# Expert tiles of a two-layer graph and mixture-of-experts kernel, as two halves of 128 rows with an expert each

## What is computed

```python
x = x + L0_gnn(layernorm(x), adj, ...)      # spectral graph block, with the eigenvectors of a 64x64 matrix
x = x + L0_ffn(layernorm(x), ...)           # 8 experts, the best two for each token
x = x + L1_gnn(layernorm(x), adj, ...)      # graph block with two batch norms
x = x + L1_ffn(layernorm(x), ...)           # a shared expert, and 8 experts, the best two for each token
# L0_ffn, for an expert e with 341 hidden units, silu and a gate product:
#   y = (silu(t @ w1[e].T) * (t @ w3[e].T)) @ w2[e].T
# L1_ffn, for an expert e with 512 hidden units, gelu and biases:
#   y = gelu(t @ W1p[e] + b1p[e]) @ W2p[e] + b2p[e]
# out[token] = gate1 * y[expert1] + gate2 * y[expert2]
```

## Time and profile before

| | |
|---|---|
| median of 3 runs | 1552.71 us (1551.8 to 1555.42) |
| the profiled execution's own time | 1541.83 us |
| its span on the core | 1540.1 us, mean granted TensorE clock 0.888 |
| PE busy | 1131.8 us (73%), weight loads 943.4 us |
| DVE busy | 917.6 us (60%) |
| ACT busy | 599.5 us (39%) |
| POOL busy | 629.1 us (41%) |
| expert part of layer 0 | 448 to 835 us |
| expert part of layer 1 | 1162 to 1506 us |

### The profile page before, as it was taken

How to read it: one execution, slowest core, us unless ns; L and a number is a source line. 1 busy time by engine, 2 the same in 40 slices (tenths; PEclk the granted TensorE clock), 3 DMA queues, 4 the chain that set the end, 5 groups by cost and what they waited for, 6 DMA issues and landing times.

```text
span 1540.1 us, 23912 instructions
## 1 busy us (share of the span) xinstructions
PE 1131.8 (73%) x6500; PEld 943.4 (61%) x6500; DVE 917.6 (60%) x3700; ACT 599.5 (39%) x1665; POOL 629.1 (41%) x611
## 2 busy tenths in 40 slices
PE   4555774688635449999996777887886339999991
PEld 3555663466524338888886434665655229999990
DVE  5776888678852126666675868756532115555673
ACT  3556554144400002222222784655432004444440
POOL 2000000334566655555544400223455665666664
PEclk9999999988756669999998898988898569999996
DMA  9991000001121112222343400000011112222446
GB/s 235 428 429 81 1 1 1 1 10 36 40 62 53 53 47 64 64 63 61 92 120 92 186 1 14 15 18 25 30 52 45 48 56 70 73 73 69 122 114 218
DMA packets 59268, 125.57 MB, mean 82 GB/s; under 512 B 13132, under 2 KB 39637, under 8 KB 57600
## 3 DMA queue, kind: packets, MB, share of 16 engines
q0 software_dynamic: 20000, 73.21, 12.7%
q1 hardware_dynamic: 39136, 50.84, 12.0%
HBM read 50.83 MB, written 74.99 MB: 82 GB/s over the span
## 4 chain that ended last, share of the span: by engine, by line
PE 58%; DVE 16%; another core or an unknown queue 9%; issue 7%; ACT 6%; DMA 2%; SPq 0%; POOL 0%; DVEq 0%; ACTq 0%; POOLq 0%
PE bank L1473 14%; PE bank L1464 8%; PE bank L1462 6%; PE bank L1461 6%; PE bank L1679 4%; PE bank L1687 4%; PE bank L195 3%; PE bank L389 3%; PE bank L1449 2%; PE bank L1634 2%; ACT work L1568 2%; DMA u<-planes 1%; PE bank L859 1%; DVE u L180 1%
## 5 line engine op out<-in xcount | busy, mean ns | idle before, releaser
L1326 POOL DMA_INDIRECT planes<-work,goal x284 | 309.4, 1089 | 279.1 <-DVE work L1385 221.8
L1473 PE MATMUL bank<-pay 128*128 128x128 f32 (+1 forms) x1988 | 289.1, 286 | 93.7 <-issue 48.5
L973 POOL DMA_INDIRECT rows<-pay,slot x256 | 253.2, 989 | 240.1 <-issue 174.5
L1473 PEld LDWEIGHTS bank<-pay 128*128 128x128 f32 (+1 forms) x1988 | 269.3, 197 | 114.2 <-issue 53.4
L1433 ACT ACTIVATE pay<-bank,pay 128x256 f32<-128x256 f32 x284 | 125.2, 475 | 219.5 <-PE bank L1464 109.9
L1429 ACT ACTIVATE pay<-bank 128x256 f32<-128x256 f32 (+1 forms) x213 | 81.6, 383 | 322.1 <-PE bank L1462 191.8
L1406 DVE TENSOR_TENSOR pay<-pay,bank 128x256 f32<-128x256 f32 (+1 forms) x213 | 89.0, 418 | 111.2 <-issue 62.2
L1464 PE MATMUL bank<-pay 128*128 128x256 f32 x568 | 140.3, 392 | 17.5 <-issue 16.2
L1461 PE MATMUL bank<-pay 128*128 128x256 f32 (+1 forms) x426 | 134.4, 398 | 12.1 <-issue 12.1
L1462 PE MATMUL bank<-pay 128*128 128x256 f32 (+1 forms) x426 | 132.9, 395 | 0.0
L1464 PEld LDWEIGHTS bank<-pay 128*128 128x128 f32 x568 | 105.9, 197 | 31.2 <-issue 17.5
(11 more groups left out here) (406 smaller groups left out, 1978.7 us busy)
## 6 DMA issues: line engine op xcount, KB each, us to landing
rows<-pay POOLq DMA_DIRECT2D x10, 3432.0 KB, 56.0
pay<-rows SPq DMA_DIRECT2D x142, 130.0 KB
u<-planes SPq DMA_DIRECT2D x64, 256.0 KB, 4.9
planes<-work,goal POOLq DMA_INDIRECT x284
wreg<-in_w SPq DMA_DIRECT2D x1, 4264.0 KB, 24.6
wreg<-in_w SPq DMA_DIRECT2D x1, 4112.0 KB, 13.4
X<-in_x SPq DMA_DIRECT2D x2, 2048.0 KB, 20.3
rows<-pay,slot POOLq DMA_INDIRECT x256
```

Source lines behind the costliest of these rows:

```text
L973: return self.nc.gpsimd.indirect_dma_start(out=xs, out_offset=bass.IndirectOffsetOnAxis(ap=self.t["slot"][:, k, q:q + 1], axis=0), in_=sel ...
L1326: nc.gpsimd.indirect_dma_start(out=planes, out_offset=bass.IndirectOffsetOnAxis(ap=t["goal"][:, j * 2 + h:j * 2 + h + 1], axis=0), in_=t[" ...
L1473: ins = T.matmul(ps[4 + j % 2][:, h * P:(h + 1) * P], t["hh"][c][0:n, h * P:(h + 1) * P], t["wst"][j % 2][0:n, at + c * P:at + (c + 1) * P ...
```

## The change

A tile keeps its 256 rows, but they are now two halves of 128 rows, each with its own expert, first row and number of real rows. A break of an expert's rows then costs part of 128 rows rather than part of 256. The worst case is 135 halves, so NT is 68 in place of 71, in both layers. PURE becomes 28 (25 before), FIRSTS 36 (39), EARLY 51 (54), which is NT - 17 as before.

- SP loads a tile by two DMAs of 128 rows, one row to a partition, with two register loads.
- The weight buffers `wst` hold two experts. In layer 0 DVE copies the first half's weights and ACT the second half's; in layer 1 DVE makes both copies, and both copies of the second bias. The second of the two buffers lies in the region `u1`, where the fetched planes now have 8 places in place of 16.
- The first products have 128 columns in place of 256, and twice as many of them. The second products, which were 128 wide already, keep their number.
- In layer 1 a Gelu covers 128 columns, and there are two for each chunk, since their bias columns differ. The Silus of layer 0 stay at 256.
- `table` counts in halves. Its comparison of 24 x 32 elements and the reduction of it are replaced by three operations on 24 elements that round up; other operations go over 2 x 24 elements.

```diff
-TS = 256
+TS = 2 * P
-NT = (2 * TOKENS + E8 * (TS - 1)) // TS
+HALVES = (2 * TOKENS + E8 * (P - 1)) // P
+NT = -(-HALVES // 2)
...
-PURE = -(-(TOKENS - E8 * (TS - 1)) // TS)
-FIRSTS = (TOKENS + E8 * (TS - 1)) // TS
-EARLY = 54
+PURE = -(-(TOKENS - E8 * (P - 1)) // P) // 2
+FIRSTS = -(-((TOKENS + E8 * (P - 1)) // P) // 2)
+EARLY = NT - 17
+YB = 8
...
-        cmp = tb["cmp"][:, 0:n * 32].rearrange("p (e i) -> p e i", i=32)
-        own.chain(V.tensor_tensor(cmp, count.unsqueeze(2).to_broadcast([P, n, 32]),
-                                  iota.unsqueeze(1).to_broadcast([P, n, 32]), ALU.is_gt))
-        own.chain(V.tensor_reduce(k, cmp, AX.X, ALU.add))
...
+        own.chain(V.tensor_scalar(k, count, 1.0 / P, (P - 1.0) / (2 * P), ALU.mult, ALU.add))
+        own.chain(V.tensor_scalar(k, k, WHOLE, None, ALU.add))
+        own.chain(V.tensor_scalar(k, k, WHOLE, None, ALU.subtract))
...
 def experts_sp(nc, sp, S, t, route, xs, planes):
...
-        at = sp.value_load(t["first"][j:j + 1, 0:1], min_val=0, max_val=E8 * CAP - TS)
+        ats = [sp.value_load(t["first"][j:j + 1, h:h + 1], min_val=0, max_val=E8 * CAP - P) for h in range(2)]
...
-        sp.dma_start(t["xin"][j % 4], xs[bass.ds(at, TS), :].rearrange("(p h) c -> p (h c)", h=2)
-                     ).then_inc(s(f"xin{j % 4}"), 16)
+        for h in range(2):
+            sp.dma_start(t["xin"][j % 4][:, h * ROW:(h + 1) * ROW], xs[bass.ds(ats[h], P), :]
+                         ).then_inc(s(f"xin{j % 4}"), 16)
...
 def experts_dve(nc, dve, own, S, t, ps, route):
     def weights(j):
...
+        if layer == 0:
+            expert = dve.value_load(t["expert"][j:j + 1, 0:1], min_val=0, max_val=E8 - 1)
+            V.tensor_copy(t["wst"][j % 2][:, 0, 0:WB[0]], W[:, bass.ds(expert * WB[0], WB[0])]).then_inc(s("w"), 1)
+            return
+        if j >= 2:
+            dve.wait_ge(s("biased"), j - 1)
+        for h in range(2):
+            expert = dve.value_load(t["expert"][j:j + 1, h:h + 1], min_val=0, max_val=E8 - 1)
+            V.tensor_copy(t["wst"][j % 2][:, h, WB[1]:WST[1]], t["b2p"][:, bass.ds(expert * P, P)]).then_inc(s("b2"), 1)
+            V.tensor_copy(t["wst"][j % 2][:, h, 0:WB[1]], W[:, bass.ds(expert * WB[1], WB[1])]).then_inc(s("w"), 1)
...
-def experts_act(nc, act, S, t, ps, layer):
+def experts_act(nc, act, S, t, ps, route):
+    def weights(j):
+        expert = act.value_load(t["expert"][j:j + 1, 1:2], min_val=0, max_val=E8 - 1)
+        if j >= 2:
+            act.wait_ge(s("down"), past("down", j - 1))
+        A.copy(t["wst"][j % 2][:, 1, 0:WB[0]], t["W"][:, bass.ds(expert * WB[0], WB[0])]).then_inc(s("second_w"), 1)
...
     for j in range(NT):
+        if layer == 0 and j + 1 < NT:
+            weights(j + 1)
...
-                A.activation(t["hh"][c], ps[c][:, 0:TS], ACT.Gelu,
-                             bias=t["wst"][j % 2][:, 2 * CH1 * P + c:2 * CH1 * P + c + 1]).then_inc(s("hh"), 1)
+                for h in range(2):
+                    ins = A.activation(t["hh"][c][:, h * P:(h + 1) * P], ps[c][:, h * P:(h + 1) * P], ACT.Gelu,
+                                       bias=t["wst"][j % 2][:, h, 2 * CH1 * P + c:2 * CH1 * P + c + 1])
+                ins.then_inc(s("hh"), 1)
...
     def up(j, c):
...
+            if layer == 0:
+                pe.wait_ge(s("second_w"), j + 1)
...
-            T.matmul(ps[c][0:n, 0:TS], w[:, a:a + n], x, start=True, stop=True)
-            T.matmul(ps[c][0:n, TS:2 * TS], w[:, HID0 + a:HID0 + a + n], x, start=True, stop=True).then_inc(s("up"), 1)
-        else:
-            T.matmul(ps[c][:, 0:TS], w[:, c * P:(c + 1) * P], x, start=True, stop=True).then_inc(s("up"), 1)
+        a, n = CH0[c] if layer == 0 else (c * P, P)
+        for h in range(2):
+            ins = T.matmul(ps[c][0:n, h * P:(h + 1) * P], w[:, h, a:a + n], x[:, h * P:(h + 1) * P], start=True, stop=True)
+            if layer == 0:
+                ins = T.matmul(ps[c][0:n, TS + h * P:TS + (h + 1) * P], w[:, h, HID0 + a:HID0 + a + n],
+                               x[:, h * P:(h + 1) * P], start=True, stop=True)
+        ins.then_inc(s("up"), 1)
```

More of the change, by code:

```diff
@@ L1015, in table @@
+        own.chain(V.tensor_copy(f[:, E8:n], k[:, 0:2 * E8]))
+        own.chain(V.tensor_tensor(k, k, f, ALU.subtract))
         own.chain(V.tensor_tensor_scan(end, self.t["ones"][:, 0:n], k, 0.0, ALU.mult, ALU.add))
+        own.inc(V.tensor_tensor(left, both(end), half, ALU.is_gt))
         own.chain(V.tensor_tensor(start, end, k, ALU.subtract))
-        own.inc(V.tensor_scalar(m, start, j, None, ALU.is_le))
-        if self.split:
-            own.chain(V.tensor_tensor(start, start, f, ALU.subtract))
@@ L1020, in table @@
-        own.chain(V.tensor_scalar(u, start, -float(TS), j256, ALU.mult, ALU.add))
-        own.chain(V.scalar_tensor_tensor(out=m, in0=end, scalar=j, in1=m, op0=ALU.is_gt, op1=ALU.mult))
-        whole = each_part(count[:, n - E8:n])
-        own.inc(V.tensor_tensor(by_part(k), whole, by_part(u), ALU.subtract))
-        own.chain(V.tensor_tensor(by_part(u), by_part(u), base, ALU.add))
-        own.inc(V.tensor_tensor(k, k, m, ALU.mult))
-        own.inc(V.tensor_tensor(u, u, m, ALU.mult))
-        own.chain(V.tensor_tensor(by_part(e), number, by_part(m), ALU.mult))
@@ L1028, in table @@
-        own.chain(V.tensor_reduce(tb["v"], k, AX.X, ALU.add))
-        V.tensor_scalar(tb["diag"], self.t["ident"], tb["v"], None, ALU.mult).then_inc(s("limits"), 1)
+        own.inc(V.tensor_tensor(m, both(start), half, ALU.is_le))
+        own.chain(V.tensor_tensor(k, start, f, ALU.subtract))
+        own.inc(V.tensor_tensor(m, m, left, ALU.mult))
+        own.chain(V.tensor_tensor(u, half, both(k), ALU.subtract))
+        own.inc(V.scalar_tensor_tensor(out=by_part(left), in0=by_part(u), scalar=-float(P), in1=each_part(count[:, 2 * E8:n]),
+                                       op0=ALU.mult, op1=ALU.add))
@@ L1887, in build @@
         t["OUT1"] = U1[:, :]
-        t["yb"] = [pairs(U1[:, T * TOK:(T + 1) * TOK]) for T in range(TILES)]
+        t["yb"] = [pairs(U1[:, T * TOK:(T + 1) * TOK]) for T in range(YB)]
         t["WS"] = W[:, E8 * WB[1]:E8 * WB[1] + WSH]
@@ L1960, in layer_view @@
             v["slot"] = slot[:, layer, :, :]
[L1961 removed]
+            v["first"], v["expert"] = ints[:, layer, 0:2], ints[:, layer, 2:4]
             v["goal"] = goal[:, layer, :]
```

135 lines of the change are left out of this document (66 added, 69 removed).

## The result

The changed kernel takes 1582.32 us, median of 4 runs (1577.0 to 1584.32), against 1554.07 us before, median of 4 (1551.8 to 1555.82): ratio 1.0177, 95% interval 1.0146 to 1.0209. It is 28 us slower where 10.6 us less were forecast, and lies outside the range.

What follows compares the result with a forecast made beforehand. PE was taken to bound the tiles outside the sends' stretch. Layer 0's -7.9, layer 1's -5.0, starts' +0.9 and +0.4 and the sends' +1.0 make -10.6 us: 1552.7 to 1542.1 us, range 1534 to 1560.

Steps and rivals of the forecast that it cites:

- Part 1: Both layers: three tiles fewer make 63 steps 60, saving 12.7 and 11.2 us, 23.9 us in all.
- Part 2: First products of 128 columns on PE: +0.08 us a tile in layer 0 (4.305), +0.055 in layer 1 (3.785).
- rival C: PE's first products: the added weight loads cost time; 0.25 of the surcharge makes 1549 us, all over 1570; chance 0.04.
- Posts "keep their number": Stretch of the sends: posts that ACT, DVE and PE wait for stay one for each chunk; no size given.
- Part 6: Stretch of the sends: layer 1's second copy lengthens POOL's indirect DMAs, by nothing to 2.1 us; +1.0 taken.
- rival B: Stretch of the sends grows: one more 6 us ACT wait in each layer, +12, 1554 us (half: 1548); chance 0.14.
- Part 3: Layer 1's DVE: second pair of copies fits; 3.80 us a tile, 3.96 with addition; -5.0 us with the tiles saved.
- rival A: Layer 1: DVE becomes the bound, 4.06 us a tile; +10.1 us in all, 1563 us; chance 0.16.
- Part 4: ACT: layer 0's weight copy (1.06 to 1.15 us) and layer 1's eight Gelus (2.1 us) are hidden.
- Rival D: ACT's copy or halved Gelus are late: 0.2 us a tile in one layer, +12, 1554 us; chance 0.05.
- Part 5: Starts: layer 1's first tile waits for another pair of copies, +0.9 us; layer 0's first load is two issues, +0.4.
- the end behind the last tile stay: 0: Behind the last tile: the time to the kernel's end does not change, 0 us.

Runs made afterwards that it cites:

- e6: Kernel before with 68 tiles in place of 71, rows beyond the 68th tile left out: 1332.61 us, ratio 0.981 to before.
- e5: Changed kernel without ACT's copy of the second half's weights in layer 0 and PE's wait for it: 1356.47 us, ratio 0.9978 to before.
- e1: Changed kernel with PE's waits in `up` reordered, the turned copy's last: 1355.04 us, ratio 0.9972 to before.
- e3: Changed kernel with DVE's turned copy ahead of the index copy: 1360.35 us, ratio 1.0007 to before.
- e15: Changed kernel with the orders of e1 and e3, the turned copy made as a product with ones: 1583.03 us, ratio 1.0189 to before.
- e14: Changed kernel with the orders of e1 and e3, and POOL's give back later in layer 0: 1595.93 us, ratio 1.0264 to before.
- e13: Changed kernel with one weight copy in place of two in layer 1, its second half's expert left out: 1340.57 us, ratio 0.9861 to before.
- e7: Changed kernel with the edits of e1 and e3 together: 1565.02 us, ratio 1.0163 to before.
- e8: The same kernel as e13 (changed, one weight copy in layer 1) on the other kind of chip: 1572.25 us, ratio 1.0207 to before.
- e10: Changed kernel with the order of e1 and POOL's give back later in layer 0: 1355.15 us, ratio 0.9976 to before, 0.9979 repeated.

## Why the prediction was wrong

**Part 1**, three tiles: right; 24.5 us by e6 against 23.9.

**Part 2** failed in a sentence: "Transposes and second products stay", and so the tile costs 4.305 in layer 0. The spacing was right (0.22 us for two instructions of 128 columns; in e5 the 24 of `up` take 2.66 us, forecast 2.67; layer 1's step is 3.79), and the surcharge of rival C is absent. But PE's own work is not all that sets layer 0's step. Even before, the first products started 0.20 us behind the turned copy's end, tile for tile: third product of `up`, Silu, gate product, index copy, turned copy, next tile. That chain was as long as PE's work. The starts in the trace of before tell it, where the busy time does not:

```profile
703.19 1.13 PE L1473 MATMUL bank<-pay 128*128 128x128 f32 x8
704.16 0.60 PE L1461 MATMUL bank<-pay 128*128 128x256 f32 x2
```

Eight instructions at 0.111 are 0.89 us, and it is 0.97 to the next tile, in all 60 steady tiles: PE waits 0.08 us for the third gate product among them. In the changed kernel on kind B this stretch is 1.03, and the 24 instructions of `up` take 2.73:

```profile
600.51 1.13 PE L1495 MATMUL bank<-u,pay 128*128 128x128 f32 x8
601.53 0.46 PE L1482 MATMUL bank<-pay 128*128 128x128 f32 x2
...
604.26 0.61 PE L1495 MATMUL bank<-pay 128*128 128x128 f32 x4
```

The prediction looked for the turned copy in layer 1 only the earlier trace rows; a busy share of 260.97 of 261 us hid a zero slack. The change then put the wait for `second_w`, in PE's queue, right behind the one for the turned copy. With the waits in the other order the step is 4.32 (e1), with the index copy behind 4.35 (e3), without ACT's copy and that wait 4.29 (e5). The term is +0.205 a tile, not +0.08: 7.4 us too little over 59 steps. That is shown.

**Posts "keep their number"**, the sentence by which Part 6 and rival B bounded the waits for POOL, and only in the stretch of the sends, is the step that cost most on the chip of the result. The count stayed, the distance to POOL's issues did not. On kind A, layer 0's steady 287.6 us are 6.3 for the first step, 59 x 4.43 = 261.4, and 19.9 of held signals. Rival B named the mechanism (waits of ACT that POOL's issues prolong) and looked for it where they were large; none of the rivals had it in the solid stretch. That PE's signal is held there is shown by e15 and by the arrival times, and that in layer 0 it goes by the distance to POOL's issue, by e14. What in the chip holds it isn't shown: neither why the chips differ, nor why in layer 1 only 2 of 45 signals at that distance are late. The kernel before sends 57 there in its layer 1, and of the 35 whose arrival its trace holds 2 are late.

**Part 3**: rival A did not come about. DVE's chain is what was worked out, 0.74 for the address load and 3.79 the step. Addition steps are 4.04, not 3.96, and about each sixth tile of layer 1 meets an issue of POOL: the steps behind the first exceed 3.79 by 3.8 us in all ahead of the last 16 and by 3.8 in those, against 0.4 and 2.7 in the forecast. Layer 1's 60 steps take 235.8 us where 229.7 were expected, 1.7 of it in the first.

**Part 4**: hidden, nearly. ACT's copy takes 1.08 us (1.06 expected), eight Gelus 2.18 (2.1). The copy costs 0.03 a tile at most. Rival D did not happen.

**Part 5**: layer 1's first tile has its second weight copy 1.24 us behind the first, for 0.9. Layer 0's start is +2.9 us on kind B for +0.4, and -1.2 on kind A; it was not pursued.

**Part 6** and "the end behind the last tile stay: 0": the issue met by a copy was sized per issue from the earlier trace rows and counted over eight tiles. It holds for all of layer 1. Rival B's own sign came in layer 1 on kind A: tile 7's finish is 117 us behind the first transposes, where it was 109.5, 2.7 of it in the first tile and 5.1 in the seven steps, for the +1.0 of Part 6. On kind A POOL still waits for tiles behind them, and the end stays (-0.4 us); on kind B it is the bound and costs 22 us (e13). This step was wrong, but not what decided on the chip of the result.

**Between the layers** the trace has +14.1 us, in code that the change leaves alone but for the table and the first tile. On kind B it is +1.0. From its first transposes to its first finish layer 1's first tile takes 8.9 us for 6.2 before, so 2.7 of the 14.1 are in the tile. On kind A the distance from layer 0's last finish to layer 1's first is 332.6 us before, 346.7 changed, 341.5 in e7, 339.8 in e8, 350.3 in e14, 346.0 in e15; there is only one trace of before on kind A, so how much of the difference is scatter is not known. Ahead of layer 1's first tile (1165.5 to 1198 us) the two longest single waits of the changed kernel have no releaser in the profile, as those for held signals have; the columns are total, times, longest:

```profile
DVE X L1804 <- remote: 10.7, 1, 10.7
ACT work L1768 <- remote: 7.4, 1, 7.4
```

against 8.7 and 4.7 for the longest of two each before (1144 to 1169 us). Why they should be longer with the changed kernel stays open.

**The balance.** From the forecast -10.6 to the trace's +35.0 are 45.6 us: 27.5 in layer 0's steady tiles (7.4 by Part 2, 19.9 by held signals), 13.2 between the layers, 6.1 in layer 1's steady tiles, 4.1 in its first seven steps, and -5.3 at the start, in layer 0's first seven steps and at the end. So the two steps that are explained make up 27 of 46 us, and without the held signals the kernel would still have been slower here.

Of the versions tried that leave nothing out, e10 (0.9976 and, again, 0.9979) and e1 (0.9972) are faster than both kernels on kind B, by 0.2 to 0.3% against before. On kind A none of those tried beats the kernel before; e1 and e10 themselves were not run there.

## What to carry to other kernels

A row of solid PE does not say that PE sets the pace: look whether its next tile starts at a fixed distance behind another engine's result, in each layer by itself. Put the wait for what comes last directly ahead of the instruction that uses it, and read in the trace's queue whether it stands there. When tiles change their length, the distance between one engine's signals and POOL's issues changes as well, and a kernel that was clear of them can come to lie on them in every second tile. Where DVE gets one more SBUF copy a tile, sum up POOL's issues at their prolonged length against the tile's, over the whole stage.

## What was not expected of the hardware

On kind A a signal of TensorE, sent 0.7 to 0.9 us behind the start of the second of two indirect DMAs of POOL, reached ACT or DVE only 1.35 to 1.6 us behind it (52 of 54 in e14); on kind B, at the same 0.81 us, it was in time. While POOL sends, the same holds for longer: of the 30 signals of PE whose arrival the trace of the changed kernel holds between 448 and 563 us, 19 are late, 6 of them by 6.5 us or more, and layer 0's first seven steps take 105.1 us. On kind B none of 40 is late in that stretch, and the seven steps take 30.9. The two kinds differ by 13 to 14% in the kernel before, and the same change is worth 1.018 on one and 1.003 on the other.
